# Six of 24 decay products on GpSimd, with a mask matmul ahead of their scores, and a new order of the pieces

## What is computed

```
x = layernorm(x + attention(x))      # 16 heads of 8, causal, power-law decay
x = layernorm(x + cross(x, ctx))     # relu(Q K^T) V over 512 context tokens
x = layernorm(x + ffn(x))            # 8 experts of 512, each token goes to its argmax
```

```
delta = (i - j).astype(jnp.float32)
decay = jnp.where(delta > 0, -decay_scale * jnp.log(jnp.maximum(delta, 1.0)), 0.0)
return jnp.where(j > i, -jnp.inf, decay)
...
scores = scores + power_law_mask(N, DECAY_SCALE)[None, None]
attn = jax.nn.softmax(scores, axis=-1)
```

## Time and profile before

| | |
|---|---|
| median of three runs | 163.81 us (162.26 to 164.03) |
| the profiled execution's own time | 163.34 us |
| its span, first to last instruction | 161.6 us |
| PE busy | 133.0 us (82%) |
| DVE busy | 126.2 us (78%) |
| ACT busy | 82.1 us (51%) |
| POOL busy | 47.5 us (29%) |
| mean granted TensorE clock | 0.968 |

### The profile page before, as it was taken

The page is one execution under the profiler, slowest core; times in us unless marked ns, Lnnn a source line. Parts: engine busy times, 40 slices in busy tenths (PEclk is TensorE's granted clock), DMA queues, the critical chain, the costliest instruction groups (busy, mean ns, idle before and its releaser), DMA issues. The chain is left out here.

```text
span 161.6 us, 3461 instructions
## 1 busy us (share of the span) xinstructions
PE 133.0 (82%) x1153; PEld 99.2 (61%) x1153; DVE 126.2 (78%) x334; ACT 82.1 (51%) x168; POOL 47.5 (29%) x59
## 2 busy tenths in 40 slices
PE   0889798677996788989989899889689999999710
PEld 0555554444654465666759678678553689999710
DVE  5863779898999999999999975856876048888850
ACT  3330004766934789676488934334040277777600
POOL 7609992000003200010010101245663004554450
PEclk9999999999999999999999999999956999999995
DMA  4774888966502561559999989940111638301100
GB/s 101 244 177 151 219 239 215 241 168 190 153 0 66 121 227 47 151 160 187 192 179 190 149 218 407 395 168 27 38 36 36 137 90 232 115 16 32 32 22 12
DMA packets 23084, 23.34 MB, mean 144 GB/s; under 512 B 2327, under 2 KB 19100, under 8 KB 22634
## 3 DMA queue, kind: packets, MB, share of 16 engines
...
...
## 5 line engine op out<-in xcount | busy, mean ns | idle before, releaser
L967 DVE TENSOR_REDUCE mx<-ps_s 128x4 f32<-128x1024 f32 (+1 forms) x24 | 28.2, 1214 | 1.4 <-PE ps_s L731 1.3
L987 DVE SCALAR_TENSOR_TENSOR es<-es,tab_sb 128x1024 f32<-128x1024 f32 x24 | 28.0, 1218 | 0.7 <-ACT es L607 0.7
L607 ACT ACTIVATE es<-ps_s 128x1024 f32<-128x1024 f32 x24 | 23.8, 1032 | 5.9 <-PE ps_s L758 5.5
L597 ACT ACTIVATE qx<-ps_m 16x1024 bf16<-16x1024 f32 x16 | 15.4, 1009 | 21.2 <-PE ps_m L742 21.1
L513 POOL TENSOR_TENSOR rstd<-var,mhalf 128x2 f32<-128x2 f32 (+1 forms) x10 | 6.5, 646 | 49.1 <-DVE var L925 49.0
L528 POOL DMA_INDIRECT out<-qx x13 | 12.8, 984 | 22.3 <-DVE qx L1110 22.3
L758 PE MATMUL ps_s<-qx,kx 128*128 128x128 bf16 (+1 forms) x128 | 14.3, 245 | 4.8 <-ACT es L607 2.7
L727 PE MATMUL ps_s<-maskb,identb 128*128 128x256 bf16 (+1 forms) x48 | 14.9, 310 | 3.9 <-DVE mx L967 2.0
L731 PE MATMUL ps_s<-kx,qx 128*128 128x256 bf16 (+1 forms) x128 | 17.3, 246 | 0.0
L666 ACT ACTIVATE es<-ps_s,b_sb 128x128 f32<-128x128 f32 x52 | 14.8, 369 | 1.7 <-PE ps_s L887 1.1
L895 PE MATMUL ps_m<-w_sb,es 128*128 128x128 f32 (+1 forms) x104 | 14.3, 281 | 1.1 <-ACT es L666 1.1
...
## 6 DMA issues: line engine op xcount, KB each, us to landing
...
```

The source lines that it names most:

```text
L597: act.activation(qx[SHIFT:SHIFT + PICKS, b, heads, :], mt[SHIFT:SHIFT + PICKS, 0:S].unsqueeze(1).to_broadcast([PICKS, GROUP, S]), ACT.Copy)\
L607: act.activation(es[:, k % EBUF, :], sc[:, :], ACT.Exp, scale=float(DK) ** -0.5).then_inc(free, 1)
L967: ins = v.tensor_reduce(mx[:, b % 2, h0:h0 + n, t], sc[:, :].rearrange("p (h k) -> p h k", h=n), AX.X, ALU.max)
L987: v.scalar_tensor_tensor(out=e, in0=e, scalar=CEIL, in1=decay[:, 0:qs].unsqueeze(1).to_broadcast([P, nh, qs]), op0=ALU.min, op1=ALU.mult). ...
```

## The change

`POOLED` names the parts 1 and 4 of the batches 0, 1 and 2. For these six `exp` pieces DVE issues nothing. GpSimd waits until ACT has read the scores and multiplies `es` by `decay`, in place, with a `tensor_tensor`, which has no clip. So that no infinite exponential arises, PE lays the mask over the diagonal block of those scores first, in two matmuls of 256 columns a piece, and the scores are added to it. `pv` waits for two counts, DVE's and GpSimd's. The addition to `x_sb` keeps its condition but stands in the pieces' order now, at `max` 2,0. The list `LATER` is new: the same 144 pieces in another order.

```
+POOLED = [(1, 4), (1, 4), (1, 4), ()]
 RESIDUAL = ("max", 2, 0)
...
-LATER = [("max", 0, 0), ("max", 0, 1), ("rouse", 1, 2), ("max", 0, 2), ("rouse", 1, 2), ("max", 0, 3), ("rouse", 1, 2), ("max", 0, 4), ("rouse", 1, 2), ("shift", 0, 0), ("max", 0, 5),
-         ("proj", 2, 0), ("exp", 0, 0), ("exp", 0, 1), ("exp", 0, 2), ("max", 1, 0), ("max", 1, 1),
...
+         ("rouse", 1, 2), ("max", 0, 4), ("rouse", 1, 2), ("shift", 0, 0), ("max", 0, 5), ("exp", 0, 0),
+         ("exp", 0, 1), ("max", 1, 0), ("proj", 2, 0), ("exp", 0, 2), ("shift", 0, 1), ("max", 1, 1),
...
+        def weights_of(b, u):
+
+            kt, _h, nh = UNITS[u]
+            qs = S - kt * P
+            e = es[:, (NU * b + u) % EBUF, :].rearrange("p (h q) -> p h q", h=nh)
+            return e, decay[:, 0:qs].unsqueeze(1).to_broadcast([P, nh, qs])
...
             for kind, b, u in order:
+                if (kind, b, u) == RESIDUAL:
+
+                    pool.wait_ge(ld_x, 16)
+                    pool.wait_ge(ld_rows, 16)
+                    filled(pool, "s", RESIDUAL)
+                    own(pool.tensor_tensor(x_sb[:, :, :], x_sb[:, :, :],
+                                           R(BO).unsqueeze(1).to_broadcast([P, TILES, D]), ALU.add), residual_ready)
+                if kind == "exp" and u in POOLED[b]:
+
+                    taken(pool, "s", (kind, b, u))
+                    e, fade = weights_of(b, u)
+                    own(pool.tensor_tensor(e, e, fade, ALU.mult), p_pooled)
...
+                    shut = u in POOLED[b]
                     for j in range(n):
                         h = h0 + j
+                        if shut and j % (512 // qs) == 0:
+                            heads = sc[:, j * qs:j * qs + 512].rearrange("p (h q) -> p h q", q=qs)
+                            pe.matmul(heads[:, :, 0:P], maskb[:, 0, :], identb[:, :].unsqueeze(1).to_broadcast([P, 512 // qs, P]),
+                                      start=True, stop=False, skip_group_check=True)
                         mm = pe.matmul(sc[:, j * qs:(j + 1) * qs], kx[:, b, h, kt * P:(kt + 1) * P],
-                                       qx[:, b, h, kt * P:S], start=True, stop=True)
+                                       qx[:, b, h, kt * P:S], start=not shut, stop=True, skip_group_check=shut)
...
-                    pe.wait_ge(p_ready, NU * b + (3 if u < 2 else 6))
+                    done_by = lambda ours: sum(len([k for k in range(NU if a < b else 3 if u < 2 else 6) if (k in POOLED[a]) == ours])
+                                               for a in range(b + 1))
+                    pe.wait_ge(p_ready, done_by(False))
+                    if done_by(True):
+                        pe.wait_ge(p_pooled, done_by(True))
...
-                if kind == "exp":
+                if kind == "exp" and u not in POOLED[b]:
                     v.wait_ge(ld_tab, 32)
```

More of the change, by code:

```diff
@@ new lines @@
+LATER = [("max", 0, 0), ("max", 0, 1), ("rouse", 1, 2), ("max", 0, 2), ("rouse", 1, 2), ("max", 0, 3),
+         ("rouse", 1, 2), ("max", 0, 4), ("rouse", 1, 2), ("shift", 0, 0), ("max", 0, 5), ("exp", 0, 0),
+         ("exp", 0, 1), ("max", 1, 0), ("proj", 2, 0), ("exp", 0, 2), ("shift", 0, 1), ("max", 1, 1),
+         ("max", 1, 2), ("ctx", 3, 0), ("exp", 0, 3), ("exp", 0, 4), ("pv", 0, 0), ("max", 1, 3), ("exp", 0, 5),
+         ("shift", 1, 0), ("pv", 0, 1), ("max", 1, 4), ("exp", 1, 0), ("pv", 0, 2), ("exp", 1, 1), ("max", 1, 5),
+         ("pv", 0, 3), ("proj", 3, 0), ("evac", 0, 0), ("max", 2, 0), ("max", 2, 1), ("shift", 1, 1),
+         ("max", 2, 2), ("turn", 0, 0), ("exp", 1, 2), ("exp", 1, 3), ("exp", 1, 4), ("back", 0, 0), ("max", 2, 3),
+         ("shift", 2, 0), ("max", 2, 4), ("out", 0, 0), ("exp", 1, 5), ("pv", 1, 0), ("pv", 1, 1), ("norm1", 0, 0),
+         ("exp", 2, 0), ("exp", 2, 1), ("pv", 1, 2), ("max", 2, 5), ("pv", 1, 3), ("evac", 1, 0), ("max", 3, 0),
+         ("max", 3, 1), ("x1t", 0, 0), ("shift", 2, 1), ("max", 3, 2), ("q2", 0, 0), ("max", 3, 3), ("exp", 2, 2),
+         ("turn", 1, 0), ("exp", 2, 3), ("relu", 0, 0), ("exp", 2, 4), ("back", 1, 0), ("shift", 3, 0),
+         ("max", 3, 4), ("pv", 2, 0), ("max", 3, 5), ("exp", 2, 5), ("pv", 2, 1), ("out", 1, 0), ("exp", 3, 0),
+         ("norm1", 1, 0), ("exp", 3, 1), ("shift", 3, 1), ("pv", 2, 2), ("pv", 2, 3), ("evac", 2, 0),
+         ("cross", 0, 0), ("exp", 3, 2), ("x1t", 1, 0), ("turn", 2, 0), ("norm2", 0, 0), ("exp", 3, 3),
+         ("q2", 1, 0), ("exp", 3, 4), ("exp", 3, 5), ("pv", 3, 0), ("back", 2, 0), ("relu", 1, 0), ("out", 2, 0),
+         ("pv", 3, 1), ("pv", 3, 2), ("norm1", 2, 0), ("pv", 3, 3), ("cross", 1, 0), ("evac", 3, 0), ("x1t", 2, 0),
+         ("turn", 3, 0), ("q2", 2, 0), ("turn", 3, 1), ("x2t", 0, 0), ("back", 3, 0), ("back", 3, 1),
[3 rows of a table added]
+         ("cross", 3, 0), ("rank", 1, 0), ("norm2", 3, 0), ("relu", 3, 1), ("route", 2, 0), ("cross", 3, 1),
+         ("rank", 2, 0), ("norm2", 3, 1), ("x2t", 3, 0), ("route", 3, 0), ("x2t", 3, 1), ("route", 3, 1),
+         ("rank", 3, 0), ("rank", 3, 1), ("warm", 3, 18)]
@@ L294, in decoder_kernel @@
         p_ready = sem("p_ready")
+        p_pooled = sem("p_pooled")
         pv_done = sem("pv_done")
@@ L502, in _ @@
             own(pool.tensor_copy(regionb[:, :], region[0:1, :]), consts)
-            pool.wait_ge(ld_x, 16)
-            pool.wait_ge(ld_rows, 16)
-            filled(pool, "s", RESIDUAL)
-            own(pool.tensor_tensor(x_sb[:, :, :], x_sb[:, :, :],
-                                   R(BO).unsqueeze(1).to_broadcast([P, TILES, D]), ALU.add), residual_ready)
-            for kind, b, u in order:
+            for kind, b, u in order:
+                if (kind, b, u) == RESIDUAL:
[8 more added lines that the diff above has]
+                    own(pool.tensor_tensor(e, e, fade, ALU.mult), p_pooled)
                 if kind in ("out", "cross"):
@@ L979, in _ @@
                                                op0=ALU.mult, op1=ALU.subtract).then_inc(mparts_ready, 1)
-                if kind == "exp":
+                if kind == "exp" and u not in POOLED[b]:
                     v.wait_ge(ld_tab, 32)
                     taken(v, "s", piece)
-                    kt, h0, nh = UNITS[u]
-                    qs = S - kt * P
-                    e = es[:, (NU * b + u) % EBUF, :].rearrange("p (h q) -> p h q", h=nh)
-                    v.scalar_tensor_tensor(out=e, in0=e, scalar=CEIL, in1=decay[:, 0:qs].unsqueeze(1).to_broadcast([P, nh, qs]),
-                                           op0=ALU.min, op1=ALU.mult).then_inc(p_ready, 1)
+                    e, fade = weights_of(b, u)
+                    v.scalar_tensor_tensor(out=e, in0=e, scalar=CEIL, in1=fade, op0=ALU.min, op1=ALU.mult).then_inc(p_ready, 1)
                 if kind == "turn":
```

20 lines of the change are left out of this document (removed), and 3 rows, old and new, of the table LATER.

## The result

| | before | after |
|---|---|---|
| median, us | 163.48 (162.26 to 164.03, 4 runs) | 169.99 (169.13 to 171.58, 4 runs) |
| ratio, 95% interval | | 1.0416 [1.0368, 1.0464] |
| profiled execution, its span | 163.34, 161.6 | 169.13, 167.3 |
| mean granted clock | 0.968 | 0.945 |

The forecast was 162.3 us with a range to 165.0. Now and then an execution runs slower, at a lower granted clock: the ratios with an interval leave such executions out, the medians do not. By the ratio the change costs 6.8 us. The profiled execution was the quickest of the four and shows 5.7 us of it in its span. In pool_alone and two_pooled the same lines have numbers lower by one (L1010, L992, L524).

A forecast was written before the change was run, and what follows sets the result against it. DVE was taken as the bound up to the last product, then PE and batch 3's hand-overs. Terms -6.8 + 3.5 + 2.3 + 0.3 = -0.7, with -0.5 for the tail, gave -1.2 us: forecast 162.3 us, range 160.2 to 165.0.

The forecast's parts named there:

- The removal: Six products at 1.14 us leave DVE before the last product: -6.8 us, with nothing hiding the gain.
- What bounds the kernel now: DVE bounds from 33.07 to 94.60 us; from 97.07 to 120.16 PE's work and batch 3's hand-overs do.
- The opening: At batch 1's first `max`, now ahead of `proj` 2, DVE idles until the loads land: +3.5 us, bounds 1.9 and 3.6.
- Less slack between pieces: Up to the last product, DVE waits for inputs that come late in the new order: +2.3 us, bounds 0.5 and 4.5.
- GpSimd's products: Six slower products on GpSimd stay off the path; contention with DVE costs +0.3 us, bounds -0.1 and 2.4.
- The masks: Twelve matmuls on PE for six pieces, 1.3 us, hidden in PE's free time: 0, or 0.7 us without that cover.
- The tail: From the last product to `warm`, only the second half's own chain is left: -0.5 us, bounds -1.5 and +1.3.
- signs set for being wrong: Slowed products beside GpSimd's, `max` 2,0 waiting for a DMA, no DMA wait around 30 us, or POOL's scatters releasing the last norm.
- GpSimd and DVE exclude each other: Rival: three DVE products lose 1.2 us each to GpSimd products, 165.6 us; both slower cases together, chance 0.16.
- Nothing is left: Rival: DVE's gaps are twice as many as found, +1.2 us, giving 163.5 us; chance 0.20.
- Batch 2's loads come late: Rival: later stores delay the loads, `max` 2,0 and all behind wait 2.9 us: 165.2; both slower cases together, chance 0.16.
- The gain comes through: Rival: loads land 1.6 us sooner and half of the small gaps close, giving 160.3 us; chance 0.22.

The follow-up runs named there:

- pool_alone: The kernel before, in its old order, with six products on GpSimd and masks ahead of their scores: 170.89 us, ratio 1.0490.
- two_pooled: The kernel before, in its old order, with only two products on GpSimd, `exp` 0,5 and `exp` 2,0: 162.49 us, ratio 0.9978.
- order_alone: The changed kernel with POOLED empty: the new order, all 24 products on DVE, no masks ahead of scores: 170.87 us, ratio 1.0472.
- write_only: The changed kernel with each of GpSimd's six products replaced by a memset of about the same length, which reads nothing: 168.44 us, ratio 1.0312.
- opening_back: The changed kernel with `proj` 2 and `exp` 0,2 put back ahead of `max` 1,0: 168.85 us, ratio 1.0408.
- the warm matmuls: 14 unread matmuls on PE ahead of `max` 1,0, added to the changed kernel (167.50 us, 1.0243) and to order_alone (170.36 us, 1.0468).
- order_both: order_alone with `proj` 2 and `exp` 0,2 ahead of `max` 1,0 again and `norm1` 0,0 and 1,0 one place later: 167.32 us, ratio 1.0276.

## Why the prediction was wrong

The profiled execution was to gain 1.2 us and lost 5.8. Several terms of the sum failed, and they are taken below in its order. The largest part of the 7.0 us between is the mutual exclusion of DVE and GpSimd, which the prediction had at +0.3.

**The removal, -6.8 us.** *What bounds the kernel now* held for before, but missed how close the next bound was. "Nothing hides that gain while DVE is the bound" is the sentence that failed: with the exclusion taken out, the removal is worth 1.1 us in the old order (with the masks' 0.9 in it) and, order_alone against write_only, 2.6 in the new one. There the traces show what became of it. DVE's waits up to the last product grow from 7.6 to 10.3 us, 2.1 of that in front of `max` 1,0 (1.68 and 3.80), since the product of `exp` 0,1 goes from just ahead of a wait for loads; another 1.2 is the `mparts` that a MEMSET holds up. The prediction had a bound for it, PE's 2.2 us of free time in front of `max` 2,0, and used it only for a rival.

**The opening, +3.5.** The mechanism was right: PE waited for the DMA and DVE behind it, and the loads came 0.9 us sooner than I had them (DVE's maximum at 33.15, not 34.1). What failed is that the step ended at the maximum. The clock fell to half and `exp` 0,2 came 1.33 us late, so DVE lost +4.7, past the bound of 3.6. Undone, it returned 1.6 us where nothing else was in the way.

**Less slack between pieces, +2.3, bounds 0.5 to 4.5.** It measured +3.6 in the change. The places I named were mostly right (`exp` 0,5, `exp` 1,0, `max` 3,4, `exp` 2,5); the norms were not among them. Without the norms' 1.2 it is +2.4, the size that I had given; what was missing is exclusion.

**GpSimd's products, +0.3, bounds to 2.4.** This is the step that went furthest wrong. The trace shows 2.6 us of stretched instructions, and removing the reads returned 1.7, with 1.2 of the stretching left. I looked for DVE products beside GpSimd products, and found one. I did not look for small `tensor_scalar` beside them (1.38 and 0.85 us of the 2.6; in opening_back a cast, 1.34), nor the other way round, at GpSimd's `rstd` beside a DVE product (1.23 us of waits, which stand even without pooled products, because the new order puts a product behind each variance where a maximum or `attn` stood).

**The masks, 0,** cost 0.9 in the old order, by the ratio. I had given 0.7 if PE's cover were gone.

**The tail, -0.5:** it measured +0.7, and +0.4 behind `warm`, where the tokens' loads are waited for. POOL's scatters did release the last norm, one of the signs set for being wrong; undoing them gained at most 0.45 up to `warm` and moved the wait behind it, so the fault was in supposing the second half's chain the only one.

**The sum** would be -6.8 + 4.7 + 3.6 + 2.6 + 0.6 + 0.7 + 0.4 = +5.8 with measured terms, in place of -1.2. Of the 7.0 us between, 2.3 are GpSimd's products and 1.3 the slack, in which the norms stand: exclusion is half of the miss. The opening has 1.2, the tail 1.6, the gaps too small for the view 0.6.

Of the rivals, *GpSimd and DVE exclude each other* was the nearest, at 165.6, with the right mechanism; it missed that the new order itself costs 7.7. *Nothing is left* named more gaps, which came, and no exclusion. *Batch 2's loads come late* was wrong: `max` 2,0 starts at 56.25 on DVE without a wait. *The gain comes through* is refuted by the result, and order_alone shows that the order doesn't close gaps but opens them.

**Open:** why the warm matmuls gave 2.8 us by the ratio in the change and nothing in order_alone; where the masks' 0.9 is lost; and most of what order_both still costs, 4.5 us, which I put down to small gaps that no run undid. A new order free of all of these faults was not tried.
